# Feature interactions of a recommender tower on one core: all five groups of x fetched as wide rows, none spread by TensorE

## What is computed

```
e  = stack([tbl_f[ids[:, f]] for f in 39], axis=1)          # 512 x 39 x 16
z0 = einsum('bid,bjd->bdij', e, e).reshape(B, 16, 39*39)
cur0 = relu(einsum('bdk,kl->bld', z0, W0))                  # 128 wide
next_h, direct0 = split(cur0, 2, axis=1)                    # 64 and 64
z1 = einsum('bid,bjd->bdij', e, next_h).reshape(B, 16, 39*64)
cur1 = relu(einsum('bdk,kl->bld', z1, W1))
z  = sum(concatenate([direct0, cur1], axis=1), axis=-1)
h  = concatenate([z, dense_ctx], axis=1)
y  = relu(relu(h @ W_top1 + b_top1) @ W_top2 + b_top2) @ W_top3
```

## Time and profile before

| | us |
|---|---|
| time, median of 3 runs (440.49 to 440.74) | 440.73 |
| the profiled execution, whole | 441.91 |
| its span, from the first to the last instruction | 439.9 |

### The profile page before, as it was taken

The page is one execution under the profiler, slowest core; times in us unless marked ns, Lnnn a source line. Parts: engine busy times, 40 slices in busy tenths (PEclk is TensorE's granted clock), DMA queues, the critical chain, the costliest instruction groups (busy, mean ns, idle before and its releaser), DMA issues.

```text
span 439.9 us, 4140 instructions
## 1 busy us (share of the span) xinstructions
PE 407.8 (93%) x1490; PEld 250.4 (57%) x1490; DVE 347.9 (79%) x196; ACT 225.7 (51%) x224; POOL 285.5 (65%) x180
## 2 busy tenths in 40 slices
PE   0578699899999999999999999999999999996997
PEld 0444356446566656565756565666656565664564
DVE  0203755799999998989898989898989898999700
ACT  3114345365565647483747474747383747462422
POOL 5787878888888888888888888888888100000000
PEclk9989799999999999999999999999999999999899
DMA  8373629696959495959595977777786858570000
GB/s 282 97 180 76 133 62 217 155 208 153 213 116 213 111 208 112 212 110 216 108 220 120 200 142 171 157 178 153 176 165 157 180 138 197 127 161 0 1 0 2
DMA packets 23988, 64.03 MB, mean 146 GB/s; under 512 B 6755, under 2 KB 14904, under 8 KB 17695
## 3 DMA queue, kind: packets, MB, share of 16 engines
q1 hardware_dynamic: 17620, 60.75, 61.7%
q0 software_dynamic: 5632, 1.35, 3.1%
q10 hardware_dynamic: 715, 1.66, 1.1%
HBM read 59.88 MB, written 3.85 MB: 145 GB/s over the span
## 4 chain that ended last, share of the span: by engine, by line
PE 76%; POOL 12%; issue 5%; DVE 3%; DMA 3%; ACT 0%; DVEq 0%
PE acc L487 15%; POOL found L266 12%; PE acc L519 12%; PE acc L512 11%; PE acc L511 11%; PE acc L530 9%; PE sums L470 6%; PE acc L526 4%; PE spread L500 3%; DVE z_lo L409 3%; DMA found<-in_table_dram,rows_sb 2%; PE spread L559 2%; PE sums L550 1%; DVE z L401 1%; DMA base_sb<-in_base_dram 1%
## 5 line engine op out<-in xcount | busy, mean ns | idle before, releaser
L266 POOL DMA_INDIRECT found<-in_table_dram,rows_sb x176 | 285.3, 1621 | 56.7 <-issue 53.3
L309 ACT ACTIVATE z_hi<-z 128x2048 fp32r<-128x2048 f32 x64 | 122.4, 1912 | 83.1 <-DVE z L401 78.4
L409 DVE TENSOR_TENSOR z_lo<-z,z_hi 128x2048 fp32r<-128x2048 f32 x64 | 146.2, 2286 | 14.6 <-ACT z_hi L309 8.8
L487 PE MATMUL acc<-squares,w 128*128 128x512 f32 (+1 forms) x224 | 111.2, 614 | 0.0
L511 PE MATMUL acc<-z_hi,w_hi 128*128 128x512 f32 x256 | 106.2, 415 | 4.5 <-issue 2.3
L401 DVE TENSOR_TENSOR z<-x_wide,h 128x2048 f32<-128x2048 f32 x48 | 109.6, 2283 | 0.0
L512 PE MATMUL acc<-z_hi,w_lo 128*128 128x512 f32 x256 | 100.2, 391 | 0.0
L401 DVE TENSOR_TENSOR z<-spread,h 128x2048 f32<-128x2048 f32 x32 | 73.2, 2286 | 20.8 <-issue 17.0
L285 ACT ACTIVATE squares<-sums 128x1024 f32<-128x1024 f32 x64 | 58.4, 913 | 59.7 <-PE sums L470 45.7
L519 PE MATMUL acc<-z_lo,w_hi 128*128 128x512 f32 x256 | 83.3, 447 | 1.8 <-DVE z_lo L409 1.8
L519 PEld LDWEIGHTS acc<-z_lo,w_hi 128*128 128x128 f32 x256 | 48.5, 191 | 26.2 <-issue 15.1
(11 more groups left out here) (44 smaller groups left out, 144.5 us busy)
## 6 DMA issues: line engine op xcount, KB each, us to landing
x_wide<-x_rows SPq DMA_DIRECT2D x96, 512.0 KB
x_parts<-x_rows SPq DMA_DIRECT2D x32, 128.0 KB
found<-in_table_dram,rows_sb POOLq DMA_INDIRECT x176
x_rows<-found SPq DMA_DIRECT2D x32, 80.4 KB
w_sb<-in_w_dram SPq DMA_DIRECT2D x1, 1280.0 KB, 6.8
x_rows<-found SPq DMA_DIRECT2D x16, 73.1 KB
z<-in_select_dram ACTq DMA_DIRECT2D x1, 576.0 KB, 7.5
wt_sb<-in_wt_dram SPq DMA_DIRECT2D x1, 512.0 KB
```

Of the source, the lines that this page charges most:

```text
L266: pool.indirect_dma_start(out=found[:, b, 2, s * D:s * D + D], out_offset=None, in_=table, in_offset=bass.IndirectOffsetOnAxis(ap=rows_sb[ ...
L309: nc.scalar.activation(z_hi[:, n % RING], z[:, n % RING], ACT.Copy).then_inc(hi_done, 1)
L409: nc.vector.tensor_tensor(z_lo[:, n % RING], z[:, n % RING], z_hi[:, n % RING], ALU.subtract).then_inc(lo_done, 1)
L487: last = nc.tensor.matmul(acc0[:, :], w0[rows, t, :], squares[rows, q % RING0, a, :], start=(t == 0), stop=(t == T0 - 1))
```

## The change

All five groups now come as wide rows, and `spread_out` is gone, with its part of the selection matrix (two of nine tiles of `select`), its semaphore, and the wait in `place` on it. The PSUM tensor stays for the dense layers, under the name `dense_acc`; one wait of the dense layer on the last multiply goes too.

A group's two fields are placed otherwise: the first ("middle") on partitions 32 to 95, by one transfer to 64 partitions (512 KB), the second ("outer") on 0 to 31 and on 96 to 127, by two transfers to 32 partitions (256 KB each). In group 2 the lower 32 partitions take their first row from the middle field, by a transfer of its own. `w1` is laid out to match.

Per chunk that is 16 transfers of wide rows in place of 6, and 5 MB in place of 3 MB. All wait on DVE's multiplies as before; DVE's multiplies of groups 0 and 3 wait on `wide_in` instead of on PE.

```
-SPREAD = [0, 3]
-WIDE = [1, 2, 4]
-SPREAD_FROM = [0, 4, 32, 12]
-WIDE_FROM = [[8, 16], [28, 35], [20, 24]]
+WIDE_FROM = [[0, 4], [8, 12], [32, 35], [16, 20], [24, 28]]
...
-        x_wide = sb("x_wide", [P, len(WIDE), QUADS * N])
+        x_wide = sb("x_wide", [P, G, QUADS * N])
...
             def widen(c, i):
                 if c:
-                    sp.wait_ge(multiplied, G * (c - 1) + WIDE[i] + 1)
-                for a, f in enumerate(WIDE_FROM[i]):
-                    sp.dma_start(x_wide[HALF * a:HALF * a + HALF, i, :],
-                                 x_rows[c % BUFS, 2, f:f + QUADS, :].rearrange("f n -> (f n)").unsqueeze(0)
-                                 .to_broadcast([HALF, QUADS * N])).then_inc(wide_in[i], 16)
+                    sp.wait_ge(multiplied, G * (c - 1) + i + 1)
+                def spread_row(parts, t, f, count):
+                    sp.dma_start(x_wide[parts, i, t * N:(t + count) * N],
+                                 x_rows[c % BUFS, 2, f:f + count, :].rearrange("f n -> (f n)").unsqueeze(0)
+                                 .to_broadcast([parts.stop - parts.start, count * N])).then_inc(wide_in[i], 16)
+                middle, outer = WIDE_FROM[i]
+                spread_row(slice(32, 96), 0, middle, QUADS)
+                if i == WHOLE:
+                    spread_row(slice(0, 32), 0, middle, 1)
+                    spread_row(slice(0, 32), 1, outer + 1, QUADS - 1)
+                else:
+                    spread_row(slice(0, 32), 0, outer, QUADS)
+                spread_row(slice(96, P), 0, outer, QUADS)
...
-                    sp.wait_ge(spread_done, len(SPREAD) * (c - BUFS + 1))
                     sp.wait_ge(summed, ND * (c - BUFS + 1))
                 place(c)
...
-            widen(0, 0)
-            widen(0, 1)
+            for i in range(3):
+                widen(0, i)
             bring(1)
-            widen(0, 2)
+            widen(0, 3)
+            widen(0, 4)
             bring(2)
...
-                if g in SPREAD:
-                    dve.wait_ge(spread_done, len(SPREAD) * c + SPREAD.index(g) + 1)
-                    x = spread[:, :, :]
-                else:
-                    dve.wait_ge(wide_in[WIDE.index(g)], 32 * (c + 1))
-                    x = x_wide[:, WIDE.index(g), :].rearrange("p (t n) -> p t n", n=N)
+                dve.wait_ge(wide_in[g], 16 * (4 if g == WHOLE else 3) * (c + 1))
+                x = x_wide[:, g, :].rearrange("p (t n) -> p t n", n=N)
...
-                    if (n + 2) % G in SPREAD and n + 2 < G * CHUNKS:
-                        spread_out(n + 2)
```

More of the change, by code:

```diff
@@ L101, in build @@
         x_rows = nc.dram_tensor("x_rows", (BUFS, 3, FR, N), F32, kind="Internal")
-        x_wide = sb("x_wide", [P, len(WIDE), QUADS * N])
+        x_wide = sb("x_wide", [P, G, QUADS * N])
         x_parts = sb("x_parts", [P, BUFS, N], F32R)
-        select_sb = sb("select_sb", [P, T0 + len(SPREAD), P], F32R)
+        select_sb = sb("select_sb", [P, T0, P], F32R)
         w0 = sb("w0", [P, T0, P])
@@ L116, in build @@
         staging = z[:, :, :, :].rearrange("p r a n -> p (r a n)")
-        select_in = staging[:, 0:(T0 + len(SPREAD)) * P]
-        w0b_sb = staging[:, (T0 + len(SPREAD)) * P:(2 * T0 + len(SPREAD)) * P]
+        select_in = staging[:, 0:T0 * P]
+        w0b_sb = staging[:, T0 * P:2 * T0 * P]
         h = sb("h", [P, 2, N])
@@ L131, in build @@
         y_sb = sb("y_sb", [1, B])
-        spread = ps("spread", [P, QUADS, N])
+        dense_acc = ps("dense_acc", [P, QUADS, N])
         sums = ps("sums", [P, 2, N])
@@ L139, in build @@
         hid2 = [z[:, 0, m, :] for m in range(M2 // P)]
-        hid1_acc = [sums[:, 0, :], sums[:, 1, :], acc0[:, :], spread[:, 0, :]]
-        hid2_acc = [spread[:, 1 + m, :] for m in range(M2 // P)]
-        y_acc = spread[0:1, 3, :]
+        hid1_acc = [sums[:, 0, :], sums[:, 1, :], acc0[:, :], dense_acc[:, 0, :]]
+        hid2_acc = [dense_acc[:, 1 + m, :] for m in range(M2 // P)]
+        y_acc = dense_acc[0:1, 3, :]
         early, late = slice(0, B - CB), slice(B - CB, B)
@@ L163, in build @@
         filler_in = sem("filler_in")
-        wide_in = [sem(f"wide_in_{i}") for i in range(len(WIDE))]
+        wide_in = [sem(f"wide_in_{i}") for i in range(G)]
         summed = sem("summed")
@@ L170, in build @@
         reduced0 = sem("reduced0")
-        spread_done = sem("spread_done")
         multiplied = sem("multiplied")
@@ L243, in _ @@
             bring(0)
-            widen(0, 0)
-            widen(0, 1)
+            for i in range(3):
+                widen(0, i)
             bring(1)
-            widen(0, 2)
+            widen(0, 3)
+            widen(0, 4)
             bring(2)
             for c in range(CHUNKS - 1):
-                for i in range(len(WIDE)):
+                for i in range(G):
                     widen(c + 1, i)
@@ L489, in contract0 @@
                 last.then_inc(contracted0, 1)
[L491 to L502, removed]
             def contract1_hi(n):
@@ L542, in hid1_of @@
                     pe.wait_ge(evicted0, CHUNKS)
-                if m == 3 and batch == early:
-                    pe.wait_ge(multiplied, G * CHUNKS)
                 if batch == late:
@@ L578, in _ @@
             add_up(0)
-            spread_out(0)
             pe.wait_ge(w0_ready, 2)
@@ L642, in layout @@
     w0a, w0b = np.zeros((2, T0 * P, P), np.float32)
-    select = np.zeros((P, T0 + len(SPREAD), P), np.float32)
+    select = np.zeros((P, T0, P), np.float32)
     mix = np.zeros((T0 * P, F), np.float32)
@@ L657, in layout @@
     from_w1 = np.asarray(inputs["L0_rec_W1"]).reshape(F, HALF, P)
[L658 to L671, removed]
+    for g in range(G):
+        middle, outer = WIDE_FROM[g]
+        for k in range(QUADS):
+            first = g == WHOLE and k == 0
+            for p in range(HALF if first else P):
+                f = (middle if first or 32 <= p < 96 else outer) + k
+                w1[p, slot1(g) + k] = from_w1[f, p % HALF]
     def by_tile(a):
@@ L679, in layout @@
         "table": np.concatenate(tables),
-        "select": select.reshape(P, (T0 + len(SPREAD)) * P),
+        "select": select.reshape(P, T0 * P),
         "w0a": by_tile(w0a),
```

## The result

The changed kernel takes 488.0 us (median of 4 runs, 484.5 to 492.4) against 440.6 beside it: 1.104 times as long, 95% interval 1.098 to 1.110. The forecast was 447.4 with a range to 462: the direction was right, the size not. The queue does bind; its loop takes 26.8 us a chunk, not 23.7. (Distances of chunks are means over chunks 3 to 14 unless a stretch is named.)

What follows compares the result with a forecast made beforehand. PE bounds the kernel, DVE right behind; after the change the wide-row queue binds at 19.3 + 4.4 = 23.7 us a chunk. Net + 6.7 us on 441.91 is 448.6, less 1.2 for the median: 447.4 us, range 429 to 462.

Steps and rivals of the forecast that it cites:

- What bounds now, and what the change takes off PE: PE paces the chunk at 22.88 us, DVE's floor is 21.57; dropping two spreads takes 0.96 us a chunk off PE.
- The mechanism: The DMA queue of wide rows becomes the bound, DVE waiting for group 0's rows; chance 0.50, 443 to 455 us.
- the hold-up of the gathers: POOL's gathers take 2.96 us instead of 1.00 beside DVE instructions reading two on-chip operands.
- SP's 16 issues: SP's issuing of wide transfers per chunk, under 10 us of a 23.7 us loop, at no cost.
- The wait for `found_lo_done`: SP's wait in `bring` for the split costs nothing, as the writes' turn comes only 15.4 us after group 0's rows.
- The loop's size: Five groups of wide rows at 3.86 us, 19.3, plus 4.4 at `bring` give 23.7 us a chunk.
- The sum: Whole kernel: 8.2 us late at chunk 14, net + 6.7 on 441.91 gives 448.6; median 1.2 lower, 447.4.
- The slow middle: Middle transfers no faster than today: 5.0 us a group, loop 29.4 us, 529 us; chance 0.18 for 455 to 529.
- The gathers' case: POOL's gathers, held up beside DVE's multiplies, become the bound: 23.1 us a chunk in nine chunks, 439 us; chance 0.14.
- compute bound: Outer transfers partly overlap, the queue's loop is 20.9 us, PE's 21.92 us a chunk rules: 427.7 us; chance 0.18.
- What would show it: Signs if right: chunks 23.3 to 24.2 us, DVE waiting on a transfer, DMA share over 0.9, wide rows 260 to 290 GB/s.
- A sign of being wrong: Signs against: a 21.9 us chunk with PE full, ACT or DVE idle at the split for a gather, wide rows at 210 GB/s.

Runs made afterwards that it cites:

- h in PSUM: The changed kernel, complete, with h kept in two free PSUM banks, so a multiply reads one operand from SBUF: 486.6 us, ratio 1.102.
- the old placement: The changed kernel, complete, five wide groups but first field on partitions 0 to 63 and second on 64 to 127: 533.2 us.
- the run with half the columns: The changed kernel, gathers kept, with half the columns of each wide transfer from chunk 1 on: 447.95 us.
- the run without gathers: The changed kernel with gathers for the first three chunks alone, later chunks working on rows already there: 479.7 us.

## Why the prediction missed

**What bounds now, and what the change takes off PE: right but for a size.** PE and DVE fill the chunk once queue and gathers are out of the way. It then takes 21.6 us, which is DVE's floor of 21.57; PE's floor, put at 21.92, is no higher. So the change takes at least 22.88 - 21.6 = 1.3 us off PE, not 0.96. The forecast doesn't hang on this term, as the queue is longer by either.

**The mechanism: right.** The queue's loop paces, DVE waits for wide rows, the gap at `bring` is in the loop, the hold-up of the gathers adds at most some 2 us (h in PSUM). SP's 16 issues take 8.8 us, hidden. The wait for `found_lo_done` costs nothing: the writes issued at 210.38 find wide rows queued until 219.5, and the late ones of 243.00 until 247.5.

**The loop's size: the failed step.** "A group: 1.36 + 2.5 = 3.86 us" adds transfers as if each ran alone. Alone they are even faster (1.30 + 2.29; 3.4 measured in one piece), yet back to back the groups take 4.06 to 4.64, on average (26.76 - 4.8) / 5 = 4.39. So the bounds were put around the wrong thing: around each transfer's rate, not around what transfers of different placement do to each other in a full queue. With the gap of 4.8 in place of 4.4 (which is a matter of where the stretch is cut) the loop is 25.1 to 28.0, against 23.7; 26.76 was measured.

**The sum.** By the text, 0.1 us in a group is 5.5 in the end. Eleven loops of 3.06 us more are 33.7. Chunk 3 came at 124.07, not 116.7: 7.4, in the loops that fill the queue. From chunk 14 to 15 1.7 came back, not 1.0, and in the last chunk 1.6, not 0.5. 33.7 + 7.4 - 0.7 - 1.1 = 39.3 is what the span is over its forecast (485.8 against 446.6). The rest of the 40.6 is the median, 0.3 above this execution where the one before lay 1.2 below.

**The rivals.** The slow middle was wrong (it runs at 404 GB/s alone) but well priced: 529 against 533.2 for the old placement. The 488.0 lies in the 455 to 529 us that it got 0.18 for, and a group is over its threshold of 4.0, but by luck: its cause is another. The gathers' case was priced at 439 and is 448: in the run with half the columns the split waited in 15 of 16 chunks, where the text gave 23.1 to nine chunks and free ones to four. That gathers would make the best case, faster by 13 us, unreachable even with a short queue was not carried into the chances: compute bound had 0.18, yet the run with half the columns, where the queue is short, takes 448 us, not 427.7, while every multiply reads two operands from SBUF.

**What would show it.** DVE's wait with a transfer as releaser came; the DMA share of a chunk is 0.92. A sign of being wrong came too, ACT's wait for gathers at the split, but the runs show that it isn't the pace. Off were the chunk (26.8, not 23.3 to 24.2), PE's idle time (3.3, not 1 to 2) and the wide rows' rate (233 to 259, not 260 to 290 GB/s).

## What to carry to other kernels

Rates of transfers measured alone don't add up in a full queue: where fast and slow placements alternate, take the mix's own rate; putting like beside like won 1.5 us a chunk here. A queue that writes, waits and reads back has a gap that is free only while the loop has slack; when a load is added, count that gap in first. When one bound is found, price the next one as well: here the gathers stood 3 us a chunk behind the queue (23.5 against 26.8), and compute 1.9 behind them (21.6).

## What was not expected of the hardware

**A gather held over several instructions.** The prediction had one gather per long DVE instruction. In the changed kernel some are held through four in a row. The timeline of POOL (start, us, instruction), and then of DVE:

```profile
208.44 1.89 POOL L271 DMA_INDIRECT found<-in_table_dram,rows_sb  x1 [0.30 <-issue]
210.63 9.35 POOL L271 DMA_INDIRECT found<-in_table_dram,rows_sb  x1 [0.30 <-issue]
```

```profile
210.22 2.28 DVE L402 TENSOR_TENSOR z<-x_wide,h 128x2048 f32<-128x2048 f32 x1
212.42 2.28 DVE L410 TENSOR_TENSOR z_lo<-z,z_hi 128x2048 fp32r<-128x2048 f32 x1
214.62 2.27 DVE L402 TENSOR_TENSOR z<-x_wide,h 128x2048 f32<-128x2048 f32 x1
216.83 2.27 DVE L410 TENSOR_TENSOR z_lo<-z,z_hi 128x2048 fp32r<-128x2048 f32 x1
219.03 0.67 DVE L421 TENSOR_REDUCE feat_a<-cur 128x32 f32<-128x512 f32 x1
```

It ends at 219.98, 0.88 us after the fourth instruction (219.10), the same distance as in the earlier trace rows. One of 9.35 us also starts at 129.75, three chunks earlier, and two of 9.34 at 290.83 and 369.38: the split's long waits, too, come in every third chunk. Why some gathers slip in between two such instructions and others don't stays open.

**The clock falls behind PE's pauses.** The mean granted clock is 0.953 where DVE and PE wait for the queue, against 0.983 before; it is 0.93 in the second long stretch above. There PE pauses for 2.84 us, from 232.67 to 235.51, and from 235.5 to 238.9 the granted clock is 0.50, the lower of its levels of 2.4 and 1.2 GHz; four matmuls then take 2.08 us that took 1.50 at 229.34. It isn't the cause: in the run without gathers PE had 3.6 idle us in a stretch of 20 even at 0.83.
